# Second attention's first two mask tiles made in the preparation by GpSimd and ScalarE, and its first transposes placed between the third head's scores

## The reference, cut to what matters

```python
def _L1_gnn_ref(x, adj_matrix, attn_mask, Wqkv, bqkv, Wout, bout, graph_bias):
    qkv = x @ Wqkv + bqkv
    q, k, v = jnp.split(qkv, 3, axis=-1)
    ...
    scores = jnp.einsum('hnd,hmd->hnm', qh, kh) * SCALE
    scores = scores + graph_bias * adj_matrix[None, :, :]
    scores = jnp.where(attn_mask[None, :, :] == 0, jnp.float32(-1000000000.0), scores)
    attn = jax.nn.softmax(scores, axis=-1)
    out = jnp.einsum('hnm,hmd->hnd', attn, vh)
    return out @ Wout + bout
...
x = x + _L1_gnn_ref(_layernorm(x, axis=-1), adj, adj, ...)
```

## Time and profile before

| | |
|---|---|
| Time, median of 3 runs | 2652.71 us (2651.66 to 2653.09) |
| The profiled execution's own time | 2650.11 us |
| Its span, first to last instruction | 2648.2 us |
| Mean granted TensorE clock | 0.968 of full |
| PE / DVE / ACT / POOL busy | 93% / 76% / 62% / 54% of the span |
| The preparation of layer 1 | about 1096 to 1177 us |
| The attention of layer 1 | about 1177 to 1885 us |

### The profile page before, as it was taken

How to read it: one execution, slowest core, us unless ns; L and a number is a source line. 1 busy time by engine, 2 the same in 40 slices (tenths; PEclk the granted TensorE clock), 3 DMA queues, 4 the chain that set the end, 5 groups by cost and what they waited for, 6 DMA issues and landing times. The chain is left out here.

```text
span 2648.2 us, 57931 instructions
## 1 busy us (share of the span) xinstructions
PE 2464.7 (93%) x20141; PEld 2009.2 (76%) x20142; DVE 2001.2 (76%) x4249; ACT 1635.2 (62%) x3100; POOL 1423.4 (54%) x1705
## 2 busy tenths in 40 slices
PE   7899999999967996389999999999699999999999
PEld 6577777777847995267777777777588888888887
DVE  6899999999943444888777777777677777777776
ACT  1777777777732332346666666666577777777775
POOL 8666666666343553622222222222378888888886
PEclk9999999999988998699999999999899999999999
DMA  3011111111073224101111111110000000000001
GB/s 102 22 64 43 44 43 57 51 44 44 23 248 131 71 69 131 56 7 43 43 43 55 48 42 42 42 42 22 7 1 0 0 0 0 0 0 0 0 0 42
DMA packets 43751, 114.01 MB, mean 43 GB/s; under 512 B 5509, under 2 KB 29806, under 8 KB 37870
## 3 DMA queue, kind: packets, MB, share of 16 engines
q1 hardware_dynamic: 38062, 97.16, 10.5%
q0 software_dynamic: 5568, 15.21, 1.9%
HBM read 99.20 MB, written 13.15 MB: 42 GB/s over the span
## 5 line engine op out<-in xcount | busy, mean ns | idle before, releaser
L2296 PE MATMUL f_pm<-f_wl,f_yt 128*128 128x256 f32 x2640 | 625.9, 380 | 1.4 <-DVE f_gg L2125 1.4
L2296 PEld LDWEIGHTS f_pm<-f_wl,f_yt 128*128 128x128 f32 x2640 | 477.2, 191 | 53.5 <-issue 1.9
L1149 POOL TENSOR_TENSOR ADJ<-ADJ,OFF 128x2708 f32<-128x2708 f32 x21 | 125.3, 5965 | 539.5 <-DVE ADJ L1229 539.5
L120 POOL TENSOR_SCALAR f_yy<-f_th,f_rs 128x255 f32<-128x255 f32 x660 | 369.7, 578 | 21.8 <-POOL f_rs L115 21.8
L570 ACT COPY a_wt<-a_tp 128x512 f32<-128x512 f32 x528 | 256.6, 566 | 144.0 <-PE a_tp L785 143.9
L2125 DVE SCALAR_TENSOR_TENSOR f_gg<-f_th,f_pm 128x512 f32<-128x512 f32 x319 | 219.0, 687 | 160.8 <-ACT f_th L2239 159.7
L683 DVE SCALAR_TENSOR_TENSOR a_lg<-a_f1s,F2S,a_fo 128x1024 f32<-128x1024 f32 (+1 forms) x264 | 296.5, 1152 | 31.6 <-PE a_fo L772 29.7
L598 POOL TENSOR_SCALAR OFF<-ADJ 128x677 bf16<-128x677 f32 x84 | 286.2, 3430 | 63.1 <-DMA ADJ<-in_adj 63.1
L1209 DVE CUSTOM_DVE_ANT_0 a_sc<-a_qk,ADJ 128x1024 f32<-128x1024 f32 (+1 forms) x264 | 288.3, 1093 | 33.8 <-PE a_qk L1319 33.8
L2239 ACT ACTIVATE f_th<-f_pm 128x512 f32<-128x512 f32 x319 | 190.6, 597 | 195.9 <-PE f_pm L2296 195.9
L1125 ACT COPY a_wt<-a_tp 128x512 f32<-128x512 f32 x264 | 154.2, 584 | 236.7 <-PE a_tp L1341 235.9
(11 more groups left out here) (326 smaller groups left out, 4521.0 us busy)
## 6 DMA issues: line engine op xcount, KB each, us to landing
ADJ<-in_adj SPq DMA_DIRECT2D x44, 1354.0 KB, 5.8
W<-in_L_ffn_w SPq DMA_DIRECT2D x32, 512.0 KB, 9.8
m_got<-YD SPq DMA_DIRECT2D x6, 768.0 KB, 10.3
out<-X SPq DMA_DIRECT2D x21, 128.0 KB
XD<-XF SPq DMA_DIRECT2D x3, 768.0 KB
m_b<-in_L_ffn_b SPq DMA_DIRECT2D x1, 2048.0 KB, 9.2
X<-in_x SPq DMA_DIRECT2D x1, 1024.0 KB, 10.4
m_rows<-XD,SLOT POOLq DMA_INDIRECT x58, 2.8
```

What stands on the lines that cost most here:

```text
L120: return eng.tensor_scalar(out, x, rs[:, 0, bass.ds(t, 1)], rs[:, 1, bass.ds(t, 1)], ALU.mult, ALU.add)
L2296: mm = pe.matmul(out, yt[:, g, r, k, :], wl[:, k, :], start=(k == 0), stop=(k == KD - 1))
```

## The change

The first mask tile no longer is VectorE's. In the preparation GpSimd makes both first tiles in eight pieces of half a tile (1354 columns), one behind the normalized rows of each of the pairs 2 to 9: for tile 0 the two halves of `off` behind pairs 2 and 3, and the two halves of the sum behind pairs 4 and 5; for tile 1 the same behind pairs 6, 7, 8 and 9. Between `off` and sum ScalarE multiplies the whole tile by `gb`, behind `full_out(3)` for tile 0 and behind `full_out(7)` for tile 1. GpSimd's first sum piece of each tile waits for that (`gb_scaled`), and ScalarE's multiply waits for both `off` pieces (`off_done`). The attention no longer makes tile 1 ahead of its loop, and counts its semaphores from there. On TensorE the first transposes of the attention, `turn(0, 0, 0, 0, 0)`, stand behind the second chunk of the third head's scores instead of behind the third chunk.

```diff
@@ layer1_prepare
         PLACES = 4 + 4 * 2
+        CUT = N // 2
+        SCALED = [3, 7]
@@ gpsimd
                 standard_rows(pool, xn[:, t % 4:t % 4 + 1, :], X[:, t:t + 1, :], rs, t).then_inc(xn_done[b], 1)
+                if b and 2 <= i < 10:
+                    tile, step = divmod(i - 2, 4)
+                    cols = slice(0, CUT) if step % 2 == 0 else slice(CUT, N)
+                    if step < 2:
+                        pool.wait_ge(adj_in[tile], 16)
+                        if tile:
+                            pool.wait_ge(bias_done[0], 1)
+                        pool.tensor_scalar(off[:, cols], adj[:, tile, cols], 0.0, MASKED, ALU.is_equal,
+                                           ALU.mult).then_inc(off_done, 1)
+                    else:
+                        pool.wait_ge(gb_scaled, tile + 1)
+                        op = pool.tensor_tensor(adj[:, tile, cols], adj[:, tile, cols], off[:, cols], ALU.add)
+                        if step == 3:
+                            op.then_inc(bias_done[tile], 1)
@@ vector
             dve.wait_ge(b_in, 32)
-            dve.wait_ge(adj_in[0], 16)
-            dve.tensor_scalar(off[:, :], adj[:, 0, :], 0.0, MASKED, ALU.is_equal, ALU.mult).then_inc(off_done, 1)
-            dve.wait_ge(gb_in, 16)
-            dve.wait_ge(off_done, 1)
-            dve.scalar_tensor_tensor(adj[:, 0, :], adj[:, 0, :], gb[:, :], off[:, :], ALU.mult,
-                                     ALU.add).then_inc(bias_done[0], 1)
@@ scalar
                 full_out(i)
+                if i in SCALED:
+                    tile = SCALED.index(i)
+                    act.wait_ge(gb_in, 16)
+                    act.wait_ge(off_done, 2 * tile + 2)
+                    act.activation(adj[:, tile, :], adj[:, tile, :], ACT.Identity, scale=gb[:, :]).then_inc(gb_scaled, 1)
@@ layer1_attention, gpsimd
-                pool.wait_ge(scaled_adj[b], i + b)
-                pool.wait_ge(off_done[b], i + b)
+                pool.wait_ge(scaled_adj[b], i)
+                pool.wait_ge(off_done[b], i)
...
-            bias(0, 1)
@@ vector
-                dve.wait_ge(off_done[b], i + b)
+                dve.wait_ge(off_done[b], i)
...
-                if h == 0:
-                    off_tile(0, 1)
-                    scale_tile(0, 1)
@@ tensor, pair
-                    turn(i, b, hp, 0, c)
+                    if c or hp or pair_before(i, b, hp):
+                        turn(i, b, hp, 0, c)
@@ tensor, ahead of the loop
                     scores((0, 0, h), c)
+                    if h == 2 and c == 1:
+                        turn(0, 0, 0, 0, 0)
```

More of the change, by code:

```diff
@@ L873, in layer1_prepare @@
         pv = ph.ps("pv", [P, 2, 512])
-        (w_in, b_in, gb_in, off_done, scaled, kept0, kept, stats, moments, inv, pchain, folded, masked,
+        (w_in, b_in, gb_in, off_done, gb_scaled, scaled, kept0, kept, stats, moments, inv, pchain, folded, masked,
          turned, xt_done, qk_mm, full_done, high_done, low_done, placed, last_placed) = ph.sems(
-            "w_in b_in gb_in off_done scaled kept0 kept stats moments inv pchain folded masked "
+            "w_in b_in gb_in off_done gb_scaled scaled kept0 kept stats moments inv pchain folded masked "
             "turned xt_done qk_mm full_done high_done low_done placed last_placed")
```

## The result

The changed kernel takes 2683.35 us (median of 4 runs, 2680.44 to 2684.17) against 2652.18 of the kernel before on the same chip: ratio 1.0115, 95% interval 1.0104 to 1.0127, 31.2 us slower. Forecast were 2669.5, range 2661 to 2680, and slower with a chance of 0.89. The direction holds, the size does not: 14 us more, outside the range. The profiled execution took 2683.17 us, its span is 2681.3, the mean clock 0.964.

What follows compares the result with a forecast made beforehand. It took TensorE to bound the attention and the preparation's end. Preparation +20.95 and attention -4.2 gave +16.75 us on the profiled 2648.2 us span, 2669.5 as a median; range 2661 to 2680.

Steps and rivals of the forecast that it cites:

- the sum pieces and their chain: Preparation: normalized rows queue behind sums awaiting ScalarE's multiply; +8.0 us at pair 5, +0.6 at pair 6, +10.3 at pair 9.
- 11 and 9: Preparation, expected sign: GpSimd waits about 11 and 9 us for ScalarE's multiply before the first and third sum piece.
- the attention: Attention start: VectorE loses two instructions, -3.2 us, and two waits under low clock go, -1.0; -4.2 in all.
- the values of pair 1 no longer wait: Preparation: PE's gap before the values of pair 1 goes because VectorE is freed of the mask tile; -1.55 us.
- the moved transposes: Attention, behind the last chunk: moving the first transposes counted as nothing, with 0.9 us kept in the bound.
- the mask piece takes 4.8 us: Preparation: each GpSimd mask piece takes 4.8 us, with 1.9 us for the lower bound.
- the port rival: Preparation: GpSimd pieces and VectorE copies exclude each other for a whole instruction; 2686 us; a part of it, chance 0.10.
- the masks: Preparation: the first two mask pieces cost nothing under about 2 us of cover; those behind pairs 6 and 7 +1.2 us.
- the likeliest case: Whole kernel: +20.95 us in the preparation and -4.2 in the attention, 2669.5 us, own range 2665 to 2675; chance 0.79.
- the clock: Preparation: PE restarts at low clock behind the gaps at pairs 5 and 9; 1.2 us each, bounds 0.84 and 2.5; +2.4.

Runs made afterwards that it cites:

- e2: The changed kernel with its mask pieces cut to 2 columns each, multiply and sums kept: 2667.63 us, ratio 1.0062 to the kernel before.
- e3: The changed kernel with ScalarE's multiply made first and masks taken from the scaled tile: 2671.31 us, ratio 1.0077 to the kernel before.
- e4: The changed kernel with the attention's first transposes back behind the third chunk: 2682.88 us, ratio 1.0121 to the kernel before.
- e7: The kernel before with only the attention's first transposes moved: 2651.76 us, ratio 0.9999 to the kernel before.
- e9: The kernel before with VectorE making tile 1's `off` ahead of its first attention score and the first transposes moved: 2647.28 us, ratio 0.9984.
- e8: The kernel before, preparation untouched, with VectorE making tile 1's `off` ahead of its first attention score: 2647.80 us, ratio 0.9983.
- e1: The changed kernel without ScalarE's multiply and with sum pieces left at 2 columns, masks kept: 2662.62 us, ratio 1.0046 to the kernel before.
- e5: The changed kernel with each GpSimd piece cut in four instructions, same work: 2672.30 us, ratio 1.0081 to the kernel before.
- e10: The changed kernel with 16 and 20 unused extra matmuls on TensorE before the transposes of pairs 5 and 9: 2680.66 us, ratio 1.0105.

## Why the prediction missed

**Right: the sum pieces and their chain.** "PE stands still for 7.7 us" at pair 5, measured 7.41; 10.3 at pair 9, measured 9.41; +0.6 at pair 6, measured none. Predicted 18.9 with contention, measured 16.8. e2 has them alone; e3 removes them by releasing the multiply early. GpSimd stood for 16.27 and 17.54 us before its sums, not 11 and 9, because TensorE, late by then, came to pairs 3 and 7 later; that cost nothing more.

**Right: the attention.** -4.2 predicted, -4.1 in the profile; the 3.39 us wait is gone and the clock stays at full (1.00) from 1219. Right too: the values of pair 1 no longer wait (-1.55), the moved transposes are worth nothing that the runs could tell (e4, e7, e9 against e8), the mask piece takes 4.8 us (4.84).

**Wrong: VectorE behind GpSimd.** The step that failed is the sentence of the port rival, "so it does not wait for the piece's end", drawn from L700 at 0.52 us. On it the masks were put at +1.2 with 2 us of cover for the first two. Measured, 8.9 us of waits for values and 4.5 of the 8.1 us of clock stand behind the mask pieces: 13.4. e1 shows the waits with the masks alone, e5 shows that their length goes with the length of GpSimd's instruction. The rival gave 2686 as a whole, the likeliest case 2669.5; 2683.35 is near the rival. It held the right rule for the copies, and got 0.10 for "a part of it". That its number comes so close is partly luck: it put the masks at 11.2 us more where 7.7 were measured and the sum pieces at 5.2 more where they came out 2.1 less, and it had no clock behind the waits for values, 4.5 us. On the sum pieces it was too dear because those do hold VectorE (single copies of 3.01 and 3.16 us), but at a time when TensorE waits for GpSimd or VectorE has time to spare (it idles 4.15 us for ScalarE soon after, at 1154.87).

The rows had it. The two copies of 1.03 us together, 0.46 and 0.54 where 0.28 is usual, met two normalizing instructions of 0.69 and 0.58 us, and each ended 0.15 us behind the one that it met, as the copy of 4.78 us did (0.14):

```profile
1119.99 0.69 POOL L120 TENSOR_SCALAR p_xn<-X,p_rs 128x256 f32<-128x256 f32 x1 [2.58 <-PE p_pt L1001]
1120.37 0.46 DVE L934 COPY KL<-p_low 64x512 f16<-64x512 f16 x1
1120.67 0.58 POOL L120 TENSOR_SCALAR p_xn<-X,p_rs 128x256 f32<-128x256 f32 x1
1120.86 0.54 DVE L934 COPY KL<-p_low 64x512 f16<-64x512 f16 x1
```

I read that as a small contention because the instruction met was small. The mask piece that L700 met was also not one of 2.5 us, as I wrote: it is recorded from 323.37 on and took 4.61. L700 works on two columns; why it was 0.36 us longer there, and why it was not held to the end, is open and was not tried. It was one case, on another operation, against the copies of this very stage.

The Trainium skill, "SBUF — State Buffer", "Who interferes with whom", says that whoever comes first has the shared ports for the whole instruction and the other blocks fully. For VectorE's copies this case agrees: 4.78 us behind a piece of 4.92. For VectorE's two-input operations see the last section.

**Too small: the clock.** 1.2 us for each of two gaps was the term, 2.4. Measured are 8.1 in four places, 1.4 to 2.7 each. Two of the places (1.8 and 2.7) exist only because of the waits for VectorE. At the two that were forecast it is 2.2 and 1.4, 3.6 for 2.4; in e2 and e5 it is 2.8 to 3.0 at each, above the upper bound of 2.5. e10 takes back 3.0 of the 3.6 us on the spot, of which little arrives at the end of the stage.

The sum: port waits +7.7 (8.9 for 1.2), clock +6.9 (8.1 and the 1.2 of the first product, for 2.4), sum pieces -2.1 (16.8 for 18.9), small gaps +0.9: 13.4, which is 34.4 less 20.95. (The 1.2 of the first product may be chance. In the prediction the upper end of the likeliest case adds up to 22.35, not 22.2; nothing hangs on it.)

## What to carry to other kernels

Before work moves to GpSimd, list what VectorE runs beside it: here a copy that met a GpSimd instruction waited for its end, so the length of one instruction counted and not the busy share; cutting the eight pieces of 3.0 and 4.8 us in four each brought 11 us back. An engine that runs ahead of its consumer through a small buffer must not be given a wait for anything later than its lead; ask in which period the released engine comes to it. A gap elsewhere (3.1 us before the first score) was the better place: 1.57 us of work there and an idle ScalarE gave 4.6 us.

## What was not expected of the hardware

A VectorE operation with two inputs in SBUF is held for less than the whole GpSimd instruction. The six-column sum at 1110.42 ended at 1114.24, 0.85 us before the mask piece beside it ended at 1115.09, while copies end 0.14 us behind theirs. In the first layer the same shows: GpSimd's mask instruction ran from 320.92 to 323.40, and the two-input operation that began at 322.68 took its usual length of 2.96 us. A third case: the subtraction L950 at 1154.87 has two such inputs and took 3.03 us, 1.80 over its usual 1.23. It ended 0.22 us behind the piece beside it (1152.87 to 1157.68), so some 1.0 us of its length lay beside the piece. Lengths on GpSimd are rough in this profile, and no run was made to test this; why it is so stays open.

How long the clock stays low behind a gap varies: after 7.41 us of idleness the next transposes and product took 2.2 us more, after 9.41 us only 1.4; in e5 after 7.83 us the product alone took 6.00 us instead of 3.62, and in e2 after 6.81 us it took 6.09, with a granted clock of 0.50 for the first 5.9 us behind the gap. From these runs a gap of 7 to 10 us can be priced only to between 1.4 and 3.0 us.
